# A fused cross-attention and expert block: all of a slot's side pieces ahead of the head's transposes

## Time and profile before

| | |
|---|---|
| median of 3 runs | 5252.0 us (5251.74 to 5252.87) |
| the profiled execution, its own time | 5251.89 us |
| its span | 5250.2 us |
| busy: PE, DVE, ACT, POOL | 64%, 75%, 46%, 27% |
| mean granted TensorE clock | 0.715 of full speed |

### The profile page before, as it was taken

The page is one execution under the profiler, slowest core; times in us unless marked ns, Lnnn a source line. Parts: engine busy times, 40 slices in busy tenths (PEclk is TensorE's granted clock), DMA queues, the critical chain, the costliest instruction groups (busy, mean ns, idle before and its releaser), DMA issues.

```text
span 5250.2 us, 64557 instructions
## 1 busy us (share of the span) xinstructions
PE 3337.5 (64%) x21126; PEld 2217.6 (42%) x21126; DVE 3946.1 (75%) x8619; ACT 2428.4 (46%) x5505; POOL 1397.6 (27%) x1125
## 2 busy tenths in 40 slices
PE   3347575665757667575665757667575665757676
PEld 2225253443625335353443625335363443525353
DVE  3698687786977778696786968778696776868753
ACT  2454444444444444544444444444544454444432
POOL 0342223223232222223223222222323222222300
PEclk7558586776858668686776858668686776858687
DMA  4000000000000000000000000000000000000000
GB/s 125 8 5 1 1 11 1 11 1 11 1 1 11 1 11 1 1 11 1 11 1 11 1 1 11 1 11 1 3 9 1 11 1 10 1 1 7 1 7 3
DMA packets 42691, 40.93 MB, mean 8 GB/s; under 512 B 6468, under 2 KB 42342, under 8 KB 42360
## 3 DMA queue, kind: packets, MB, share of 16 engines
q1 hardware_dynamic: 42360, 36.85, 2.3%
HBM read 32.64 MB, written 4.19 MB: 7 GB/s over the span
## 4 chain that ended last, share of the span: by engine, by line
DVE 44%; PE 26%; issue 12%; ACT 12%; POOL 3%; DVEq 0%; POOLq 0%; ACTq 0%; DMA 0%; SPq 0%
DVE banks L713 7%; DVE row_negmax L1252 5%; DVE masks L704 4%; PE banks L287 4%; DVE u L941 4%; DVE steps L729 4%; PE banks L356 4%; PE banks L265 3%; PE banks L789 3%; DVE c L675 3%; PE banks L320 3%; DVE eg_eth L959 2%; PE banks L278 2%; DVE o L968 2%; DVE steps L735 2%
## 5 line engine op out<-in xcount | busy, mean ns | idle before, releaser
L618 POOL TENSOR_TENSOR steps<-slope,rises 128x512 f32<-128x512 f32 x256 | 302.6, 1182 | 2951.3 <-DVE masks L704 2357.2
L713 DVE COPY_PREDICATED banks<-masks,banks 128x448 f32<-128x448 int16 (+5 forms) x1536 | 1028.1, 669 | 28.3
L789 PE MATMUL banks<-xn,w 128*128 128x256 f16 x6912 | 852.5, 285 | 111.2 <-ACT h L861 111.2
L789 PEld LDWEIGHTS banks<-xn,w 128*128 128x128 f16 x6912 | 693.7, 102 | 273.8 <-ACT h L861 139.1
L704 DVE TENSOR_SCALAR masks<-shift 128x512 int16<-128x512 int16 x1536 | 334.7, 288 | 438.5 <-ACT shift L546 434.8
L1252 DVE TENSOR_REDUCE row_negmax<-banks 128x4 f32<-128x1024 f32 x256 | 306.1, 1215 | 159.7 <-PE banks L341 159.7
L632 POOL TENSOR_TENSOR partial<-partial,core_scores 128x512 f32<-128x512 f32 x256 | 357.2, 1395 | 0.1
L675 DVE TENSOR_TENSOR_SCAN c<-gate,cap 128x514 f32<-128x514 f32 x256 | 341.6, 1335 | 1.0 <-ACT gate L530 1.0
L443 PE MATMUL banks<-table,core_queries 64*128 64x256 f16 x512 | 124.6, 333 | 339.5 <-ACT slope L593 339.5
L861 ACT ACTIVATE h<-banks,b 128x256 f32<-128x256 f32 x576 | 238.6, 465 | 216.3 <-PE banks L789 216.1
L622 POOL TENSOR_TENSOR partial<-slope,neg_rest 128x512 f32<-128x512 f32 x256 | 330.4, 1291 | 2.1 <-DVE negmax L735 2.1
(11 more groups left out here) (262 smaller groups left out, 7462.7 us busy)
## 6 DMA issues: line engine op xcount, KB each, us to landing
stage<-in_L_ffn_w SPq DMA_DIRECT2D x16, 512.0 KB, 5.5
ahead<-in_ctx SPq DMA_DIRECT2D x32, 128.0 KB, 2.2
ahead<-in_x SPq DMA_DIRECT2D x32, 128.0 KB, 2.3
u<-in_ctx SPq DMA_DIRECT2D x32, 128.0 KB
x<-in_x SPq DMA_DIRECT2D x32, 128.0 KB
out<-x SPq DMA_DIRECT2D x32, 128.0 KB, 1.8
stage<-in_L_ffn_w SPq DMA_DIRECT2D x8, 256.0 KB, 6.1
stage<-in_L_ffn_sw SPq DMA_DIRECT2D x2, 512.0 KB, 4.4
```

What stands on the lines that cost most here:

```text
L618: nc.gpsimd.tensor_tensor(k.steps[:, g % 2], k.slope[:], k.rises[:, g % 2], ALU.mult)\
L713: move = nc.vector.copy_predicated(tab[:, :, 0:S - b], k.masks[:, n, :, 0:S - b], tab[:, :, b:S])
L789: last = nc.tensor.matmul(k.bank[bank][:, f * S:(f + 1) * S], w[:, e, a, c, par, f * P:(f + 1) * P], k.x_parts[:, b, c, :], start=(n == 0) ...
```

## The change

`FIRST` becomes a copy of `PIECES`. In `core_tensor` all side pieces of the slot are issued ahead of the wait for the exponentials, the four transposes and the core scores of head s+2; in `core_scalar` all side pieces are issued ahead of the copy of the transposed probabilities. The second loop over side pieces runs zero times on both engines. No instruction is added or removed, and no wait is changed: only the place in TensorE's and in ScalarE's queue moves.

```diff
-FIRST = [(2 * n + 1) // 3 for n in PIECES]
+FIRST = list(PIECES)
```

## The result

| | before | after |
|---|---|---|
| median | 5251.87 us (5251.5 to 5252.87) | 5305.08 us (5302.45 to 5307.8) |
| ratio after / before | | 1.0101 (95%: 1.0084 to 1.0119) |
| the profiled execution and its span | 5251.89, 5250.2 us | 5307.8, 5306.1 us |

The change costs 53 us, where 38 were forecast; 5305 lies within the range of 5264 to 5318.

What follows compares the result with a forecast made beforehand. No engine alone was taken as the bound; what counts is VectorE's idle time, chiefly waiting for ScalarE's shift. Slot terms gave +2.5 us per batch: 14 x 2.5 + 3.1 = 38 us on 5251.9, so 5290, range 5264 to 5318.

Steps and rivals of the forecast that it cites:

- slot 0 +1.3: End of side slot 0: transposes and copy follow the gate logits, slope 3 us later, 1.7 us cover used up; +1.3 us.
- slot 6 +0.5: End of side slot 6: transposes hide beside two ScalarE copies, the moved copy does not; +0.5 us, bounds 0.4 and 0.9.
- slot 13 -0.7: Side slot 13: transposes leave the chain of exponentials, the 1.2 us lead partly returns; -0.7 us, bounds -1.2 and 0.
- Slot 5 +0.3: Side slot 5, TensorE full: table product and next query projection come about 0.85 us late; +0.3 us, bounds 0 and 0.6.
- slot 11 +0.5: End of side slot 11: transposes hide beside the last stack copies, the copy stands alone; +0.5 us, bounds 0.4 and 1.0.
- wrong if slot 14 gets shorter: Sign in the profile after: the prediction is wrong if slots 8 and 14 get shorter; slot 14 was priced +0.2 us.
- Slot 1 was forecast at 0: Side slot 1: slope comes later, but VectorE reaches its next masks over 3 us after, so slope and table stay hidden.
- Slots 7 and 15 were forecast at 0: Slot 7: transposes and copy fit ahead of VectorE's last move, by thin margins; slot 15: the moved pieces are empty.
- The eight terms of the sum: Prices for slots 0, 5, 6, 8, 9, 11, 13 and 14, summing to +2.7 us per batch, 2.5 unrounded.
- The faster rival: Slots 8, 9, 13, 14: exponentials come earlier and the copy costs nothing; -2.7 us a batch, -40, so 5212; chance 0.06.
- Nothing moves: Copies find another gap, faster clock covers slot 0, slots 6, 8, 11 partly charged; 5252 to 5260 us; chance 0.06.
- The late table is not hidden: Slots 1 to 5 pay for late slope and table, transposes at 1.2 GHz everywhere; +4.7 per batch, 5320 us; chance 0.16.

## Why the prediction was right, and where it was not

**The mechanism was right.** Slope and shift stand behind TensorE's late transposes and the copy: 105 waits forecast and 105 found, their total forecast at 470 and found at 478.7. Putting the copy behind slope and shift in the changed kernel, and nothing else, takes the new waits and all 53 us away. Not all of that is this mechanism: slots 7 and 15 got shorter too, by 0.5 and 0.6, and slots 9 and 14 longer.

**The slots, forecast against found:** slot 0 +1.3 / +1.36; slot 6 +0.5 / +0.70 (the transposes ran at 1.2 GHz there, not at 2.4, and took 1.06); slot 8 +0.7 / +0.73; slot 9 -0.1 / -0.04; slot 13 -0.7 / -0.82; slot 14 +0.2 / +0.07; slots 2, 3, 4, 10 and 12 as forecast. Slot 5 +0.3 / -0.05 lies just below its bounds, and slot 11 +0.5 / +0.82 within them. Slot 14 is luck: seven of its 14 batches are 0.5 shorter, three 0.1 longer and four about 1.1 longer, so the sign "wrong if slot 14 gets shorter" came true in half of them.

**Slot 1 was forecast at 0 and is +0.93.** This is the largest term that the sum had wrong. I had priced its own order and had not asked in what state ScalarE enters it. Before, ScalarE left slot 0 with 1.7 us in hand, and its exponentials were done when the gate's logits came. Now it has no lead. VectorE idles 1.07 us instead of 0.67 for the gate's exponentials, and its next small instructions fall differently against GpSimd's. Slot 1 of the changed kernel, VectorE's and GpSimd's rows, and then VectorE's of the kernel before:

```profile
2606.75 0.17 DVE L975 RECIPROCAL esum<-esum 128x2 f32<-128x2 f32 x1 [1.07 <-ACT escore L867]
...
2606.95 0.98 DVE L976 TENSOR_TENSOR escore<-escore,esum 128x16 f32<-128x16 f32 x1
...
2607.96 1.19 DVE L978 TENSOR_TENSOR ebiased<-escore,gate_b 128x16 f32<-128x16 f32 x1
```

```profile
2606.76 1.13 POOL L628 TENSOR_TENSOR neg_rest<-shift,c 128x512 f32<-128x512 bf16 x1 [0.17 <-POOL partial L622]
2607.85 1.26 POOL L632 TENSOR_TENSOR partial<-partial,core_scores 128x512 f32<-128x512 f32 x1
```

```profile
2583.00 0.17 DVE L975 RECIPROCAL esum<-esum 128x2 f32<-128x2 f32 x1 [0.67 <-ACT escore L867]
2583.20 0.17 DVE L976 TENSOR_TENSOR escore<-escore,esum 128x16 f32<-128x16 f32 x1
...
2583.41 0.17 DVE L978 TENSOR_TENSOR ebiased<-escore,gate_b 128x16 f32<-128x16 f32 x1
```

Two VectorE instructions that took 0.17 us before last 0.98 and 1.19, and each ends 0.04 us after a GpSimd one (2606.95 + 0.98 = 2607.93, GpSimd's 2607.89; 2609.15 and 2609.11). Before, two others were held in this way (L983 and L984, 0.51 and 1.19 instead of 0.17 and 0.23), 1.3 us in all against 1.8 now. Together with 0.4 of longer wait that makes the 0.93. The Trainium skill, "SBUF — State Buffer" (section "SBUF: two separate sides"), describes the port that these two engines share as an exclusive lock held for a whole instruction; these rows agree. That slot 0 makes slot 1's length is shown by three runs: slot 0 alone changed (+0.93), and twice slot 0 alone excepted (0.00). With the copy last, slot 1 stays at +0.92: the shift itself is in time there, but the copy still waits for slot 0's late transposes and holds up ScalarE's start of slot 1. Its row there, and VectorE's wait for the exponentials is 1.12 us again:

```profile
2570.04 0.60 ACT L594 ACTIVATE core_pT<-banks 128x512 f32<-128x512 f32 x1 [1.26 <-PE banks L265]
```

**Slots 7 and 15 were forecast at 0** and are +0.53 and -0.87. Their work is the same; their clock is not. In the seven batches in which slot 7 takes 18.8 us, its mean granted clock is 0.50, and in the other seven it is 0.52 to 0.57. Slot 15 began at the full clock in about every second batch before, and in all 14 after. The first microseconds of two slots 15 of the kernel before, one of 18.8 us and one of 17.0, show it:

```profile
2541.75:2546.00 4.25, 4.25 (x28) 2.44 (x26) 3.21 (x11) 3.28 (x7) 2.55 (x3) 0.50 0.01 2
...
2856.24:2860.50 4.26, 2.38 (x28) 1.36 (x26) 4.16 (x14) 3.92 (x10) 2.56 (x3) 1.00 0.17 54
```

28 matmuls each, 1.2 GHz in the one and 2.4 GHz in the other, 4.25 us and 2.38 us of TensorE.

**Where the forecast fell short.** The eight terms of the sum were found at 2.8 us a batch, against 2.7. (The prediction took 2.5 "with the unrounded terms", which it doesn't give; by the rounded ones the forecast is +41, and the high bounds add up to 5.5, not 5.6.) The rest of the +3.4 found is slots 1, 7 and 15, all put at 0: together +0.6, after +0.93 and +0.53 have been set against -0.87. In the profiled executions the 14 batches are longer by 48 us, and what stands behind them by 7, where the forecast had 3. So the +38 is low by slot 1 and by the end of the program, and it is by luck that slots 7 and 15 partly cancel.

**Adding up was the weak step.** I added the slots up and multiplied by 15. The two kernels with added reductions show that a cost measured in its own slot can't be carried over to the time here: +0.7 us a batch is absorbed, +2.1 becomes +3.3. With slot 0's split restored, 2.1 us a batch came back, and only about half of it in the time. The lengths of slots 7, 9, 14 and 15 take up or give back 0.5 to 2 us in a batch, with different granted clocks. Many batches fall on the same few lengths: all lie within 0.3 of 314.0 with one reduction, most neighbouring pairs of before make 628.0 to 628.3, so 314.0 each, and 317.4 to 317.5 is found in eight of 14 of the changed kernel, in seven with three reductions, and in five with all but slot 0. The kernels with a late copy and changed splits don't keep to them: their batches run from 310.0 to 314.9. The mean of the changed kernel, +3.4 a batch, is about the step from 314.0 to 317.4, so that the nearness of +38 to +53 says little for a sum of small terms.

The Trainium skill ("TensorE: Matmul & The Clock Gate", Part 4) says that the full clock doesn't engage for transposes. This stays contradicted: in slot 14 of the changed kernel four take 0.66 us at a granted clock of 1.00, and in slot 6 four take 1.06 us at the low clock. The page's 275 ns are of bf16 transposes, these are of fp32. Other matmuls stand around them, so whether transposes alone would raise the clock no run here shows.

```profile
2880.34 0.66 PE L265 MATMUL banks<-ident,core_prob 128*128 128x128 f32 x4
...
2880.47 0.38 ACT L1178 ACTIVATE u<-banks 128x256 f32<-128x256 f32 x1 [1.19 <-PE banks L356]
...
2881.03 0.60 ACT L585 ACTIVATE core_pT<-banks 128x512 f32<-128x512 f32 x1 [0.17 <-PE banks L265]
2881.53 0.59 ACT L593 ACTIVATE slope<-banks 128x512 f32<-128x512 f32 x1
```

**The faster rival** (the early exponentials win) is real in its mechanism and falls in its condition, as put: slot 13 is 0.8 to 1.0 shorter in the three kernels that change it with the copy ahead of the slope, and 1.2 to 1.3 with the copy last, the figure that the rival gave. With the copy last everywhere and slot 0 as before, it makes the best version, 5237. But its -40 us shrinks to -14: slots 9 and 14 don't give their part in the mean (+0.38 and -0.05). They do give it where the clock is higher: in that kernel slot 9 takes 15.8 to 16.5 us at a mean clock of 0.67 to 0.69 and 17.1 at 0.55 to 0.59, slot 14 takes 16.1 at 0.79 and 18.2 at 0.53, and before they took 16.4 and 17.4. Beside these, slot 11 takes 0.5, slot 15 gives 1.2 that nobody had counted, and the end of the program takes 10 us.

**The other two rivals.** "Nothing moves" had slot 0 covered by a faster clock and slots 6, 8 and 11 only partly charged; slot 0's transposes took 1.09 us, at the low clock, and all four slots paid. "The late table is not hidden" gave 5320, and the measured time lies between it and the forecast, but not by its mechanism: slots 2, 3 and 4 have their lengths of before, and slot 5 is not longer. Of its parts, transposes at the low clock came true in slot 6, for 0.2, and in slot 11 in half of the batches, where they cost nothing more (23.1 us with them, 23.3 without); and slot 7 lost its margin in half of the batches.

**What stays open.** That slots of the same work and different length differ in their granted clock is shown in the rows; why the batch settles at such lengths, and why the end of the program is 3 or 10 us longer in some kernels, is not: no run set the clock by itself. Nor is it settled why slot 11 is 0.4 to 0.5 longer in four of the five kernels with the copy last, two of which left its split alone, and not in the fifth, which has the old split everywhere.

## What to carry to other kernels

In a hand-made interleaving, price a moved instruction by what the engine does right behind it: here a copy of 0.6 us ahead of the instruction that releases the bounding engine cost its wait and itself, and behind it next to nothing in the slots. A lead of one engine at the end of a stage is cover for the next stage too; ask who spends it. And where a loop has stretches at both TensorE clocks, add a small known cost (0.7 us a turn, then three times that) to the kernel before, and see whether times add up, before a sum of small terms is believed. Look at the end of the program too: a stretch that an edit doesn't touch can change by as much as the edit is worth.

## What the runs showed of the hardware that was not expected

- A fixed 0.686 us of VectorE work per batch changed the time by -2.7 us in all (within its interval of nothing), and three of them by +48.6 us. What answers are stretches that the edit doesn't touch, at another granted clock (slot 15: 0.76 against 0.67, 17.02 against 18.78 us).
- Kernels with different slots have batches of the same length: 317.46 us in the changed one, 317.45 with slot 0 restored, 317.43 with three reductions.
- The stretch behind the last core head, the same 1280 matmuls in every kernel, took 261 us at a granted clock of 0.78 in the kernel before, and 271 at 0.72 in one whose batches have another order.
- VectorE instructions of 0.17 us on 16 columns lasted up to 1.19 us beside a GpSimd instruction, and ended 0.04 us after it.
